# Gating by one SiLU pass, x loaded two batches ahead, and the preparation and shared tiles of a selective scan moved to other slots

## What is computed

```python
# per layer; x: (8, 1024, 256)
xn = layernorm(x) * ln_g + ln_b
xp = xn @ pw.T + pb
z  = silu(xp)
xf = softplus(xp @ cfw.T + cfb);  x1 = ssm(xf)
xb = softplus(xp[:, ::-1] @ cbw.T + cbb);  x2 = ssm(xb)[:, ::-1]
x  = x1 * z + x2 * z + x

def ssm(x):                       # 16 states n, both directions use the same weights
    delta, Bm, Cm = split(x @ dbc_w.T, [32, 16, 16])
    delta = softplus(delta @ dtp_w.T + dtp_b)
    # h[t] = exp(delta[t] * A[n]) * h[t-1] + delta[t] * Bm[t, n] * x[t]
    # y[t] = sum over n of h[t, n] * Cm[t, n]
    return y + x * Dp             # A = -exp(A_log)
```

## Time and profile before

| | |
|---|---|
| time, median of 3 runs | 21882.45 us (21880.83 to 21883.69) |
| the profiled execution | 21919.67 us, its span 21917.8 us |
| instructions | 192,168 |
| granted PE clock, mean | 0.969 |
| first scan starts | 113.4 us after the span's start |
| data read from and written to HBM | 3836.9 MB, 125.8 MB |

### The profile page before, as it was taken

One profiled execution on the slowest core, in us unless ns is written; L12 is line 12 of the kernel. 1 busy time (PEld: TensorE's weight loads), 2 busy tenths in 40 slices (PEclk: granted clock), 3 DMA queues, 4 the chain that ended last, 5 costly groups with the idle time before them and its releaser, 6 DMA issues.

```text
span 21917.8 us, 192168 instructions
## 1 busy us (share of the span) xinstructions
PE 18480.5 (84%) x45506; PEld 7633.0 (35%) x46368; DVE 20326.0 (93%) x11964; ACT 11667.5 (53%) x12349; POOL 20726.1 (95%) x8269
## 2 busy tenths in 40 slices
PE   7888888888888888888888888888888888888887
PEld 3333333333333333333333333333333333333333
DVE  7999999999999999999999999999999999999999
ACT  5555555555555555555555555555555555555554
POOL 8999999999999999999999999999999999999999
PEclk9999999999999999999999999999999999999999
DMA  4555555555555555555555555555555555555555
GB/s 151 185 183 178 188 183 180 182 181 184 182 184 183 176 187 182 181 183 183 181 181 184 180 183 184 180 181 180 186 180 181 186 181 181 183 183 182 184 184 179
DMA packets 1125763, 3978.56 MB, mean 182 GB/s; under 512 B 148992, under 2 KB 159744, under 8 KB 1124352
## 3 DMA queue, kind: packets, MB, share of 16 engines
q1 hardware_dynamic: 1073664, 3926.33, 52.5%
q10 hardware_dynamic: 50688, 36.88, 0.7%
HBM read 3836.89 MB, written 125.83 MB: 181 GB/s over the span
## 4 chain that ended last, share of the span: by engine, by line
issue 32%; PE 21%; POOL 19%; DVE 18%; DMA 6%; ACT 2%; DVEq 1%; POOLq 0%; ACTq 0%; SPq 0%
DVE ring L834 13%; POOL ring L364 12%; PE y L677 11%; PE bank L695 6%; DVE bv L818 5%; PE bv L667 3%; DMA c<-c_rows 3%; DMA pre<-out_dram 2%; POOL delta L404 2%; POOL u L412 2%; POOL parts L394 1%; POOL v L372 1%; PE y L688 1%; ACT dA L503 1%; DVE w L848 1%
## 5 line engine op out<-in xcount | busy, mean ns | idle before, releaser
L364 POOL TENSOR_TENSOR ring<-ring,c 128x1024 f32<-128x1024 f32 x6144 | 14310.1, 2357 | 407.9 <-DVE ring L834 366.9
L677 PE MATMUL y<-ring,ident 128*128 128x512 f32 x24576 | 11793.3, 606 | 460.0 <-DVE z L840 272.3
L834 DVE TENSOR_TENSOR_SCAN ring<-dA,bv 128x1024 f32<-128x1024 f32 x5376 | 12027.8, 2271 | 159.2 <-ACT dA L503 58.9
L818 DVE TENSOR_TENSOR bv<-u,bv 128x1024 f32<-128x1024 f32 x5376 | 6391.9, 1215 | 1288.7 <-PE bv L667 1051.8
L503 ACT ACTIVATE dA<-delta,a_step 128x1024 f32<-128x1024 f32 x5376 | 5971.8, 1143 | 1726.0 <-DVE ring L834 1573.1
L677 PEld LDWEIGHTS y<-ring,ident 128*128 128x128 f32 x24576 | 4763.0, 195 | 4804.5 <-issue 3593.2
L667 PE MATMUL bv<-parts,select 128*128 128x512 bf16 x9890 | 3130.8, 392 | 2521.7 <-DVE ring L834 2448.0
L503 ACT ACTIVATE bv<-delta,a_step 128x1024 f32<-128x1024 f32 x768 | 856.8, 1116 | 4004.2 <-DVE ring L834 4004.2
L667 PEld LDWEIGHTS bv<-parts,select 128*128 128x128 bf16 x10752 | 776.3, 100 | 6297.3 <-DVE ring L834 5287.5
L372 POOL TENSOR_TENSOR v<-u,v 128x1024 f32<-128x1024 f32 x768 | 1809.2, 2356 | 652.8 <-DMA v<-c_rows 652.6
L834 DVE TENSOR_TENSOR_SCAN ring<-bv,v 128x1024 f32<-128x1024 f32 x768 | 1738.9, 2264 | 0.0
(11 more groups left out here) (66 smaller groups left out, 11966.2 us busy)
## 6 DMA issues: line engine op xcount, KB each, us to landing
c<-c_rows SPq DMA_DIRECT2D x6144, 512.0 KB, 4.4
v<-c_rows SPq DMA_DIRECT2D x768, 512.0 KB, 5.8
out_dram<-z SPq DMA_DIRECT2D x96, 1024.0 KB, 7.8
pre<-out_dram SPq DMA_DIRECT2D x88, 1024.0 KB, 7.6
w<-out_dram SPq DMA_DIRECT2D x88, 1024.0 KB, 6.5
c_rows<-dbc ACTq DMA_DIRECT2D x192, 128.0 KB, 2.2
pre<-in_x_dram SPq DMA_DIRECT2D x8, 1024.0 KB, 7.9
w<-in_x_dram SPq DMA_DIRECT2D x8, 1024.0 KB, 6.4
```

What stands on the lines that cost most here:

```text
L364: nc.gpsimd.tensor_tensor(ring[k % NR][:], ring[k % NR][:], c_sb[k % NC][:], ALU.mult).then_inc(p_ready, 1)
L677: mm = pe.matmul(y[:, half(h)], ident[:], ring[k % NR][:, half(h)], start=(k % HALF_TILES == 0), stop=(k % HALF_TILES == HALF_TILES - 1), ...
L818: nc.vector.tensor_tensor(bv[k % 2][:], u_of(d, s)[:, c, :], bv[k % 2][:], ALU.mult).then_inc(v_ready, 1)
L834: nc.vector.tensor_tensor_scan(h, a, b, 0.0, ALU.mult, ALU.add).then_inc(h_ready, 1)
```

## The change

- The gate is one Silu pass of ACT over z in place, at ACT's slot 37 of the preparation, after both convolutions have read z. The table set `silu_and_others` is loaded ahead of it and the old set behind it. ACT's three passes and POOL's multiplication go, with their semaphores.
- The scratch tiles of the two directions are swapped: the direction prepared first uses `pre`, the second `tmp`. So `pre` is free after `DELTA_AT[0]`, and x of the iteration after the next is loaded into it at slot 52, instead of x of the next at the start of the iteration.
- `SHARED`, the lead of B's load (4 to 5 slots) and of POOL's multiplication (7 to 6), the slots of nearly all pieces of the preparation, of the skips, of the store (16 to 12), of w's load (50 to 59) and of the weights (54 to 55) are others. `HELD` is the number of slots at the start of a half in which its first sum is held back.
- In ACT's slot the pieces of the weights come ahead of the exponential. A few waits move with the scratch tiles.

```diff
+SILU_TABLES = "silu_and_others"
-    SHARED = (7, 15, 23, 31, 39, 47, 55, 63)
-    B_AHEAD, V_AHEAD = 4, 7
-    LAG, HELD = 5, 3
+    SHARED = (9, 19, 23, 29, 35, 45, 55, 59)
+    B_AHEAD, V_AHEAD = 5, 6
+    LAG, HELD = 5, 2
-    MEAN_AT, CENTRE_AT, SQUARE_AT = (1, 7), (9, 11), (8, 11)
-    VAR_AT, RSTD_AT, NORM_AT = (9, 11), (10, 12), (9, 12)
-    PROJ_AT, XP_AT = (15, 17, 19, 19), (16, 16, 20, 20)
-    CONV_AT = ((21, 23, 25, 27), (29, 31, 33, 35))
-    CONV_OUT_AT = ((22, 22, 28, 29), (29, 30, 32, 34))
-    XS_LOG_AT, XS_AT = ((29, 32), (35, 35)), (34, 39)
-    DBC_AT, DBC_OUT_AT = ((37, 39), (44, 46)), ((37, 39), (50, 50))
-    DTP_AT, DTP_OUT_AT = ((41, 41, 42, 43), (49, 49, 51, 51)), ((40, 40, 42, 42), (51, 51, 52, 52))
-    HI_AT, REST_AT, MID_AT, PARTS_AT = (41, 51), (45, 54), (48, 54), (47, 56)
-    DELTA_LOG_AT, DELTA_AT, U_AT = ((43, 46), (53, 55)), (46, 56), (48, 57)
-    DIAG_AT, A_STEP_AT = 53, 40
-    GATE_AT, GATE_MUL_AT = (2, 3, 9), 5
-    STORE_AT = 16
-    W_AT = 54
-    SKIPS = ((9, 7), (39, 46))
+    MEAN_AT, CENTRE_AT, SQUARE_AT = (3, 4), (8, 10), (7, 10)
+    VAR_AT, RSTD_AT, NORM_AT = (9, 11), (11, 15), (9, 16)
+    PROJ_AT, XP_AT = (15, 15, 19, 19), (16, 16, 19, 19)
+    CONV_AT = ((22, 23, 25, 27), (29, 31, 33, 35))
+    CONV_OUT_AT = ((21, 23, 28, 29), (29, 30, 33, 34))
+    XS_LOG_AT, XS_AT = ((31, 32), (35, 35)), (35, 39)
+    DBC_AT, DBC_OUT_AT = ((37, 39), (47, 49)), ((37, 39), (47, 48))
+    DTP_AT, DTP_OUT_AT = ((41, 41, 41, 42), (49, 51, 51, 51)), ((40, 41, 42, 42), (50, 50, 52, 52))
+    HI_AT, REST_AT, MID_AT, PARTS_AT = (40, 49), (44, 53), (45, 57), (47, 55)
+    DELTA_LOG_AT, DELTA_AT, U_AT = ((43, 47), (55, 55)), (47, 55), (47, 57)
+    DIAG_AT, A_STEP_AT = 49, 53
+    GATE_AT = 37
+    STORE_AT, LOADX_AT, LOADW_AT = 12, 52, 59
+    W_AT = 55
+    SKIPS = ((13, 9), (51, 55))
-        scratch = (tmp, pre)
+        scratch = (pre, tmp)
...
             def load_x(n, src, b):
-                sp.wait_ge(delta_ready, n * 2)
+                if not early(n, 1):
+                    sp.wait_ge(delta_ready, (n - 1) * 2 + 1)
                 sp.dma_start(pre[:], src[b]).then_inc(x_loaded, 16)
...
-                if more:
-                    load_x(it + 1, next_src, (b + 1) % NB)
...
-                    if k == 50:
+                    if k == LOADW_AT:
                         load_w(it, src, s, b)
+                    if k == LOADX_AT and ahead:
+                        if b < NB - 2:
+                            load_x(it + 2, src, b + 2)
+                        else:
+                            load_x(it + 2, out_d, b + 2 - NB)
             load_x(0, x_d, 0)
+            load_x(1, x_d, 1)
...
-            def gate(k, it, s):                      # POOL
-                if k == GATE_MUL_AT:
-                    pool.wait_ge(gate_sig, it + 1)
-                    nc.gpsimd.tensor_tensor(z[s][:], z[s][:], tmp[:], ALU.mult).then_inc(gate_ready, 1)
...
-            def gate(k, it, s):                      # ACT, three passes
...
                             if i == 0 and j == 0:
                                 act.wait_ge(proj_ready, n * FILLS + FILLS)
+                                act.wait_ge(var_ready, n * 2 + 2)
+                            if i == 0 and j == 1:
                                 act.wait_ge(normed, n * 2 + 2)
-                            if i == 0 and j == 1:
-                                act.wait_ge(var_ready, n * 2 + 2)
...
+                if k == GATE_AT:
+                    nc.scalar.preload_act_table_set(SILU_TABLES)
+                    act.wait_ge(conv_ready, n * (2 * FILLS) + 2 * FILLS)
+                    nc.scalar.activation(z[s][:], z[s][:], ACT.Silu).then_inc(gate_ready, 1)
+                    nc.scalar.preload_act_table_set(TABLES)
...
             def rstd(n, h):
                 act.wait_ge(var_ready, n * 2 + (h + 1))
-                act.wait_ge(gate_ready, n)
+                act.wait_ge(delta_ready, n * 2)
...
+                    weights(k - AHEAD - W_AT)
                     tile_exp(it, k, s)
-                    gate(k, it, s)
-                    weights(k - AHEAD - W_AT)
```

More of the change, by code:

```diff
@@ L175, in conv_seq_kernel @@
         ln_done = sem("ln_done")
-        gate_exp = sem("gate_exp")
-        gate_log = sem("gate_log")
-        gate_sig = sem("gate_sig")
         gate_ready = sem("gate_ready")
@@ L306, in store, with step @@
                 sp.dma_start(out_d[b], z[s][:]).then_inc(stored, 16)
-            def step(it, b, src, next_src, more=True):
+            def step(it, b, src, ahead=True):
                 s = b % 2
-                if more:
-                    load_x(it + 1, next_src, (b + 1) % NB)
                 sp.wait_ge(c_stored, it * 32 + 32)
@@ L323, in step @@
                         store(it - 1, 1 - s, (b - 1) % NB)
-                    if k == 50:
+                    if k == LOADW_AT:
                         load_w(it, src, s, b)
+                    if k == LOADX_AT and ahead:
[3 more added lines that the diff above has]
+                            load_x(it + 2, out_d, b + 2 - NB)
             load_x(0, x_d, 0)
+            load_x(1, x_d, 1)
             for b in range(NB):
-                step(b, b, x_d, x_d if b < NB - 1 else out_d)
+                step(b, b, x_d)
             with sp.Fori(1, LAYERS - 1) as layer:
                 for b in range(NB):
-                    step(layer * NB + b, b, out_d, out_d)
+                    step(layer * NB + b, b, out_d)
             last = (LAYERS - 1) * NB
             for b in range(NB):
-                step(last + b, b, out_d, out_d, b < NB - 1)
+                step(last + b, b, out_d, b < NB - 2)
             store(last + NB - 1, 1, NB - 1)
@@ L515, in log1p @@
                 nc.scalar.activation(scratch[j][:], scratch[j][:], ACT.Ln, bias=1.0).then_inc(ln_done, 1)
-            def gate(k, it, s):
[L518 to L527, removed]
             def prepare(k, n, s):
```

## The result

The changed kernel takes 21360.09 us (median of 4 runs, 21353.13 to 21364.14), 522 us less than the kernel before; the ratio is 0.9761, with a 95% interval of 0.9744 to 0.9778. The forecast was 21,440 us, in a range of 21,080 to 21,760.

A forecast was written before the change was run, and what follows sets the result against it. DVE, held up by PE, and chains from DVE through POOL's u were taken to bound a batch: 218.7 against 223.3 us, -4.6 x 96 = -442, +5 at the start, 21,483 profiled, said as 21,440; range 21,080 to 21,760.

The forecast's parts named there:

- The gate, 0 on the path: POOL's multiplication at slot 5, 4.5 us a batch, goes; counted as 0, since no chain leaving DVE later contains it.
- The lump: Silu pass and two table loads at ScalarE's slot 40, 4.5 us between two tile exponentials; 0 taken.
- The cover: Slack between exponential 41 being ready on ScalarE (10.1) and scan 41 starting (12.8): 2.7 us.
- The rival of the slow switch: Table switches between running ScalarE passes stop it for long; at 7 us each +375 us, about 22,260; chance 0.09.
- x, -3.5 us: PE's mean at slot 1 no longer waits for x, removing 3.5 us a batch of DVE's waiting.
- PE's lumps: Even slots have room for about 0.5 us of fill, odd about 2.8; slot 46 -2.98, 22 +1.25, 51 +1.0.
- The rows: B rows loaded one slot earlier, used one later: POOL's 6.8 us of waits should shrink; landing taken as 5.8 us.
- The sign that POOL would wait before tiles 23 and 59: POOL's waits for v rows would be concentrated before these two tiles, with none of length elsewhere.
- The chain: Longest run from DVE through POOL to the end of u: by the row of 59, 218.5 us.
- The batch counted from: One undisturbed batch read in the trace before, 223.3 us, from which the gain of 4.6 us was taken.
- Start: The first preparation, which nothing covers, gets the lump: +4.5 us once.
- The second rival: Clumps return at slots 4, 22, 51 and ScalarE's 40: 221.5 to 222.5 us a batch, -130 to -200, 21,700; chance 0.16.

The follow-up runs named there:

- a4: The changed kernel with the old gate put back (three ScalarE passes, POOL's multiplication, no table switch): 21,346 us.
- b2: The changed kernel with POOL normalizing one column of each half instead of 512, at slots 9 and 16, ahead of scan 38: 21,348 us.
- b1: The kernel before with POOL's gate multiplication cut to one column of 1024: 21,731 against 21,825 us.
- b5: The changed kernel with six more table loads ahead of the Silu pass: 22,163 us.
- a2: The kernel before with only the scratch tiles swapped and x loaded two batches ahead at slot 52: 21,682 against 21,807 us.
- a3: The kernel before with both the Silu gate and x loaded two batches ahead, all other slots old: 21,490 us, ratio 0.9856.
- a1: The kernel before with the gate's change alone (one Silu pass, two table loads): 21,695 against 21,807 us.
- c4: a3 with the B rows loaded 5 slots ahead instead of 4 and multiplied 6 ahead instead of 7: 21,445 us.
- b3: The changed kernel with POOL's sum for the first direction's delta at slot 47, behind scan 38, cut to one column of 1024: 21,277 us.

## Why the prediction was right

The forecast was -4.6 us a batch; the layers show -5.7. The steps hold in part, and that the total came so near has luck in it: the gate was worth more than 0 in the kernel before, x alone less than its term, the chain at the head was another, and the batch counted from was a short one. By the prediction's steps:

- *The gate, 0 on the path.* In the changed kernel right (a4, b2). In the kernel before wrong by 1.0 us a batch (b1): the routes from a lagging POOL by ScalarE to PE and DVE weren't counted. "No chain that leaves DVE for POOL after slot 5 contains it" was true and not enough.
- *The lump.* 4.5 us, as taken, and no wait at scan 41. The cover was mis-sized: 0.7 us instead of 2.7 (b5). I had let ScalarE come to the slot free, waiting for PE; in the trace it comes there from two softplus passes and two exponentials. The Silu pass took 1.91 us where 1.89 was taken. The rival of the slow switch had the mechanism right, and b5 is what it would have looked like.
- *x, -3.5 us.* The wait went. Alone it brought 1.3 us a batch on its chip (a2), and 2.1 with the gate changed as well (a3 beside a1).
- *PE's lumps.* The best term. DVE waits for PE 4.0 us a batch, as forecast, with 1.25 us behind slot 22 to the digit; slot 51 cost 1.6 instead of 1.0. The rest, 0.7 us at tile 2 and 0.4 at tile 62, wasn't forecast; the sum had taken the small wait at tile 2 as gone. The timeline after:

```profile
5724.48 1.23 DVE L801 TENSOR_TENSOR bv<-u,bv 128x1024 f32<-128x1024 f32 x1 [1.26 <-PE bv L650]
...
5823.19 1.23 DVE L801 TENSOR_TENSOR bv<-u,bv 128x1024 f32<-128x1024 f32 x1 [1.61 <-PE bv L650]
```

- *The rows.* The lead is worth about 0.5 us a batch (c4), far from the 6.8 that POOL had idled; the sum gave it no term of its own. The landing was taken as 5.8 us for both critical rows, 23 and 59. Both landed faster, in 4.0 us (medians over the batches), so the chains through them were counted 1.8 us too long there. Only the row of tile 19, issued 2.3 us behind the store that now stands at slot 12, took 8.5, and POOL never waited for it. The sign that POOL would wait before tiles 23 and 59 half failed: it waits 0.8 us a batch at 23, 0.4 at 35 and 0.1 at 59. One instance of tile 19's row, then of tile 59's:

```profile
v<-c_rows SPq DMA_DIRECT2D x1, 512.0 KB, 8.5
```

```profile
v<-c_rows SPq DMA_DIRECT2D x1, 512.0 KB, 3.8
```

- *The chain.* The row of 59 was to be the longest, 218.5. The longest is by scan 38, which I had not added up. By the prediction's own terms it is 218.4: between scans 38 and 44 DVE takes 19.0 us and POOL 20.8. So the total of the sum was right with the wrong chain at its head, which is luck. From DVE's, POOL's and SP's timelines of the batch after, the chains are 219.0 by scan 38, 218.3 by the row of 59 (DVE to scan 55 took 189.7 us, 1.8 more than summed, which the faster landing made up), 217.2 by scan 44 and 216.9 by the row of 23. b3 shows the second taking over.
- *The batch counted from.* The sum ended near what it aimed at, 218.7 against 219.1 for ordinary batches. It started from 223.3, one batch read in the trace before, while these average 225.7 there. The batch read is the second of its layer. The second, fourth and sixth take 224.1 us on average, with 1.7 us of waiting at tile 52, the route of b1, where the one read has 0.2. The first, third and fifth take 227.6, with 4.9 us at tile 4 and 1.7 at tile 8, where it has 3.5 and none. This is most of what the forecast fell short. The batch with weights work gained 6.9 us, like the others, and the one behind it nothing.
- *Start.* The first scan is at 110.1 us, 3.3 earlier and not 5 later.
- *The second rival.* Its price doesn't follow from its batch: 221.5 to 222.5 against 223.3 is -77 to -173 us, not -130 to -200.

## What to carry to other kernels

Where two engines are over 90% busy and hand work to each other, neither share tells what an instruction is worth. Find the places where one has just waited for the other, add up chains between them, and look at every switch point: work ahead of the last meeting is free (b2, a4) unless a third engine waits for its lag in between (b1: 1.0 us), and work behind it counts until the next chain takes over (b3: 0.7 of 4.4 us). Count from an average over many batches, not from one. A piece put into an in-order engine costs what it exceeds the slot's room (b5), and the room must be read from what that engine does just before, not from its share.

## What the runs showed of the hardware

- A switch of table set in mid-stream took 1.28 us and 0.01 to 0.02 us around it, with passes right before and behind. The Trainium skill, "ScalarE: Activation LUTs", What ACT_TABLE_LOAD costs, adds a drain of 1.38 us for each switch. No such gap stands here in 192 loads, nor in the loads back to back of b5 (0.01 us apart); the measurement decides.
- After the change a row of B, 512 KB, landed in 4.0 us at tiles 23 and 59, where SP had issued nothing for 7 us or more in the batch read, and in 8.5 us at tile 19, where a store of 1 MB and a row of C had been issued within 2.3 us ahead of it (medians over 96 batches).
- The kernel before took 21,807, 21,825 and 21,917 us on three chips, 0.5% apart; the changed one 21,360 in the result and 21,367 on the last of these. Why the first differs more is open.
